# A second wait inside each pair's eight gathers, in the first layer of a graph network

## The reference

```
h   = relu(layernorm(x))
ef  = (relu(edge_attr @ We1 + be1) @ We2 + be2) * sigmoid(edge_weight @ Wt + bt)
msg = relu(concat([h[src], ef]) @ Wn1 + bn1) @ Wn2 + bn2
x   = x + (segment_sum(msg, dst) + h)                      # first layer
h   = relu(layernorm(x))
agg = segment_sum(h[src], dst)
x   = x + relu(relu((h + agg) @ W1 + b1) @ W2 + b2)        # second layer
```

## Time and profile before

| | us |
|---|---|
| median of 3 runs | 3862.44 (3859.89 to 3878.18) |
| the profiled execution: device time | 3848.36 |
| its span on the core | 3846.6 |
| mean granted TensorE clock | 0.797 |
| first gather of the program, last one | 47.7, 3797.0 |

### The profile page before, as it was taken

One profiled execution on the slowest core, in us unless ns is written; L12 is line 12 of the kernel. 1 busy time (PEld: TensorE's weight loads), 2 busy tenths in 40 slices (PEclk: granted clock), 3 DMA queues, 4 the chain that ended last, 5 costly groups with the idle time before them and its releaser, 6 DMA issues.

```text
span 3846.6 us, 58359 instructions
## 1 busy us (share of the span) xinstructions
PE 2746.8 (71%) x14587; PEld 1705.2 (44%) x14588; DVE 1970.9 (51%) x4080; ACT 1013.4 (26%) x1000; POOL 2069.2 (54%) x2109
## 2 busy tenths in 40 slices
PE   4877677767677777778777877776663766667667
PEld 3444444444344444435444444443342544455445
DVE  8654555555555555555555555564674333333333
ACT  3332333323233333323233332322231101111112
POOL 7655555555455555555555554545336455555553
PEclk8788888887888788878887887877886767777778
DMA  5433333333333333333334343333213333333331
GB/s 169 123 119 111 113 120 110 111 120 105 117 101 120 110 109 116 120 107 115 112 114 116 104 124 109 114 109 104 79 51 128 99 96 122 123 120 98 111 121 63
DMA packets 234934, 426.49 MB, mean 111 GB/s; under 512 B 86462, under 2 KB 147470, under 8 KB 234542
## 3 DMA queue, kind: packets, MB, share of 16 engines
q0 software_dynamic: 74160, 151.46, 15.3%
q1 hardware_dynamic: 109552, 178.49, 14.1%
q10 hardware_dynamic: 50928, 93.34, 6.8%
HBM read 363.64 MB, written 59.42 MB: 110 GB/s over the span
## 4 chain that ended last, share of the span: by engine, by line
issue 27%; PE 21%; SPq 20%; DVE 13%; another core or an unknown queue 10%; DVEq 7%; DMA 1%; ACT 0%; POOL 0%; ACTq 0%
SPq L486 14%; PE ps L1000 9%; PE ps L900 4%; SPq L482 3%; DVE nodes L1270 3%; PE ps L858 3%; DVEq L1194 2%; PE ps L868 2%; DVEq L1250 1%; DVE arena L1270 1%; DVEq L1267 1%; PE ps L990 1%; DVE big L1220 1%; DVE hot L1225 1%
## 5 line engine op out<-in xcount | busy, mean ns | idle before, releaser
L592 POOL DMA_INDIRECT big<-table,idx x2064 | 2001.8, 970 | 1670.8 <-issue 593.7
L900 PE MATMUL ps<-nodes 128*128 128x500 bf16 x1280 | 433.6, 460 | 324.5 <-DVE nodes L1270 191.4
L858 PE MATMUL ps<-arena,we 128*128 128x512 f32 x784 | 496.0, 762 | 28.5 <-issue 16.2
L713 ACT ACTIVATE big<-big 128x1024 f32<-128x1024 f32 x196 | 207.1, 1057 | 1151.1 <-DVE big L1220 828.3
L1270 DVE TENSOR_SCALAR nodes<-iota_k,win_off,nodes 128x500 bf16<-128x500 f16 x1280 | 461.6, 413 | 0.5 <-issue 0.5
L879 PE MATMUL ps<-hot,big 128*128 128x64 f32 x3136 | 414.2, 288 | 52.8 <-issue 28.2
L879 PEld LDWEIGHTS ps<-hot,big 128*128 128x128 f32 x3136 | 406.0, 208 | 57.6 <-issue 55.7
L1220 DVE TENSOR_TENSOR big<-ps,big 128x1024 f32<-128x1024 f32 x180 | 219.5, 1219 | 354.0 <-issue 287.4
L849 PE MATMUL ps<-arena,we 64*128 64x512 f32 x784 | 258.0, 727 | 199.9 <-DMA arena<-in_ea 187.0
L1267 DVE TENSOR_TENSOR nodes<-iota_b,nodes 128x384 bf16<-128x384 f16 (+1 forms) x492 | 245.5, 499 | 223.0 <-remote 182.6
L1202 DVE TENSOR_TENSOR acc<-ps,acc 128x128 f32 x392 | 114.1, 291 | 458.4 <-remote 398.6
(11 more groups left out here) (152 smaller groups left out, 2604.4 us busy)
## 6 DMA issues: line engine op xcount, KB each, us to landing
arena<-in_ew SPq DMA_DIRECT2D x196, 512.0 KB
arena<-in_ea SPq DMA_DIRECT2D x196, 256.0 KB
counts_d<-arena ACTq DMA_DIRECT2D x192, 245.0 KB
acc<-counts_d ACTq DMA_DIRECT2D x15, 2940.0 KB
big<-table,idx POOLq DMA_INDIRECT x2064
nodes<-table SPq DMA_DIRECT2D x2048, 0.5 KB
table<-big SPq DMA_DIRECT2D x7, 672.0 KB, 3.0
idx<-in_src SPq DMA_DIRECT2D x260, 4.0 KB
```

What stands on the lines that cost most here:

```text
L592: pool.indirect_dma_start(to(u, q, t)[0:n], None, table, bass.IndirectOffsetOnAxis(ap=idx[0:n, u, at:at + 1], axis=0))\
L858: i = pe.matmul(p_ef[q], we2[:, :], hid[:, q, :], start=True, stop=True)
L900: m = pe.matmul(to, hots[:, t, :], keys[:, t, :], start=False, stop=True, skip_group_check=True)
```

## The change

GpSimd's eight gathers of a pair are split by block. The first four are issued after the three waits of before. Ahead of the second four there is now a wait for `agg_mm >= 4 b + u - 2` and one more raising of `pairs_begun`, on which no one waits. The count P-2 is reached when TensorE has done the sums of pair P-3, in its step P. The last two bodies get no new wait; pair 195's short tile and the tile left out of the 16 special pairs are as before. The helper `gather_rest` gives way to `gather_half`. The second layer isn't touched.

```diff
+            def gather_half(b, u, q, last):
+                if last and u == RING - 1:
+                    gather_block(table0, to_rows, u, q, gathered, EDGE_TILES - (NTILE - (2 - q) * TB))
+                elif isinstance(b, int) and (b * RING + u, q) in FETCHED:
+                    gather_block(table0, to_rows, u, q, gathered, TB, (TB - 1) * q)
+                else:
+                    gather_block(table0, to_rows, u, q, gathered)
...
                     if not free:
                         pool.wait_ge(ef_mm, b * (2 * RING) + 2 * u)
                     pool.sem_inc(pairs_begun, 1)
-                    if last and u == RING - 1:
-                        gather_last(table0, to_rows, gathered)
-                    elif isinstance(b, int) and b * RING + u in dict(FETCHED):
-                        gather_rest(table0, to_rows, u, dict(FETCHED)[b * RING + u], gathered)
-                    else:
-                        gather_pair(table0, to_rows, u, gathered)
+                    gather_half(b, u, 0, last)
+                    if not free:
+                        pool.wait_ge(agg_mm, b * RING + (u - 2))
+                    pool.sem_inc(pairs_begun, 1)
+                    gather_half(b, u, 1, last)
```

More of the change, by code:

```diff
@@ L599, in gather_pair @@
                     gather_block(table, to, u, q, landed)
-            def gather_rest(table, to, u, half, landed):
-                for q in (0, 1):
-                    gather_block(table, to, u, q, landed, TB, (TB - 1) * q if q == half else None)
             def gather_last(table, to, landed):
```

## The result

The changed kernel took **3701.7 us** (median of 6 runs, 3693.1 to 3717.9), the kernel before 3861.2 us (6 runs, 3849.4 to 3878.2): a ratio of **0.959**, 95% interval 0.956 to 0.962. The forecast was 3798 with a range of 3690 to 3950. The sign is right and the time lies in the range, but the gain is 160 us where 64 were forecast.

The account below looks back on a forecast made before the run. GpSimd's gather batches were taken to hold up news between engines. 46 bodies x (2.3 us gained - 0.9 us second pauses) = 64 us, from 3848.4 to 3784, plus 14 for the median: 3798 us, range 3690 to 3950.

Parts of the forecast that it names:

- The hold: First layer: during gather batches and 1.6 to 1.9 us after, little news passes between engines; 8.2 of a light pair's 12.6 us.
- The rule of the Trainium skill: A DMA never contends with a compute engine, so gathers wouldn't make the 2.9 us gaps and a split would give nothing.
- The new wait is found unmet: Ahead of the fifth gather: news of the sums comes only once gathers stop, so GpSimd pauses 2.9 us there.
- the extra instructions are hidden: GpSimd's added wait and increment per pair hide in the 0.30 us gap between gathers; bound 110 us if not.
- The light pairs: Sums' news passes in the middle of a pair, so TensorE starts the heavy pair 4.9 us sooner.
- Second pauses: GpSimd pauses 2.9 us again at the border in one light pair of ten: 0.9 us per body, between 0 and 8.7.
- The heavy pair: Needs about 9.8 us outside holds, before and after; ends at 53.9 us after the change, 56.2 before.
- The last eight pairs: The last two bodies have no new wait and were left out of the sum: change of 0.
- Both pauses: Rival: edge products regularly unknown after the second four, light pair 15.2 us instead of 12.6; 3996 or 4115 us; chance 0.30.
- Short batches not held: Rival: half of the lone batches of four pass without a hold; about 5 us per body, 3632 us; chance 0.10.
- Nothing: Rival: sums known in time, or the pause merely moves into the pair with batches of eight; 3862 us; chance 0.17.
- the tail: Time a hold lasts after a gather batch's end: 1.6 to 1.9 us, taken as 1.7.

Follow-up runs that it names:

- e13: Changed kernel with four small GpSimd instructions, which wait for nobody, in place of the second wait: ratio 0.953.
- the fifth chip: Chip of the fifth group: kernel before 2834.6 us; changed kernel with two or seven small GpSimd instructions in place of the second wait: 1.076 and 1.262.
- e1: Changed kernel with the second wait on the sums of one pair earlier, always known already: ratio 1.002.
- e8: Changed kernel with the second wait on the products of this pair's attributes instead of the sums: ratio 1.002.
- e15: The changed kernel itself once more, on the fourth group's chip: ratio 0.955.
- e11: Changed kernel with the second wait in the three light pairs of each body alone: ratio 0.989.
- e10: Changed kernel with the second wait in the heavy pair of each body alone: ratio 0.980.
- e2: Kernel before with all eight gathers of a pair behind the sums, in place of the wait for the edge products: ratio 0.966.
- e14: Changed kernel, the heavy pair's second four gathers waiting for the end of its own counting instead of the sums: ratio 0.976.
- e9: Changed kernel with both waits in the last two bodies too: ratio 0.951.
- e12: Changed kernel without SyncE's single-row transfers and with both waits in the last two bodies too: 3561.1 us, ratio 0.939.
- e7: Kernel before with first-layer gathers of 16 rows instead of 128 from pair 4 on: ratio 1.032.
- e6: SyncE's single-row transfers left out, GpSimd gathering those tiles: kernel before 0.986, changed kernel 0.947.

## Why the prediction was right or wrong

**The hold: right.** In the changed kernel too VectorE and SyncE move together just before GpSimd resumes; SyncE's twelves stay slow; e13 shows that a stop without any news of its own is enough, and the fifth chip speaks for it from the other side: without the hold the stop is a loss. The rule of the Trainium skill that was weighed ("SBUF — State Buffer", Who interferes with whom), by which the gaps would not be of the gathers' making, gave "nothing": it doesn't cover this.

**The new wait is found unmet, and the extra instructions are hidden: right.** Gaps stand in the middle of light pairs and hardly at a border; e1 and e8 price the instructions at 0.2% with an interval around zero, where the bound was 110 us.

**The light pairs: near.** Forecast -4.9 us, with the second pauses +0.9, so -4.0; measured -2.7. *Second pauses* came out smaller than the term: besides the pairs behind a heavy one, which have both pauses as forecast (33 of 45), only 5 of 135 pairs have one in the middle and one at the border, 5 x 2.5 / 45 = 0.3 us per body for 0.9. The pauses in the middle last 2.3 to 2.7 us on average where 2.9 was taken. One thing wasn't in the sum at all: SyncE. Its fetches beside gathers are so slow that the attributes behind them came late for 8.3 us of a body, 4.0 before. The prediction had read SyncE as slow in each hold and didn't follow its queue to the attributes. In the two kernels without fetches the light pairs fell from 34.6 to 31.2 us, 3.4 less (on two chips whose kernels before differ by 0.4%). But leaving the fetches out is worth no more to the changed kernel (0.947 for 0.959) than to the one before (0.986), so it isn't shown that the later attributes cost the change much.

**The heavy pair: the step that failed.** By the prediction "it needed about 9.8 us outside holds" before, and it gave the pair the same 9.8 us outside holds after the change. Work done in a hold thus counted as nothing, and the pair grew from 18.4 to 21.0: +2.6. Measured: 19.2 to 18.0, -1.2 (18.3 in e15, on a chip where the kernel before has no profile). This term alone is 3.8 us x 46 = 175 us off; the light pairs (1.3 x 46 = 60) and the last eight pairs (27) were off to the other side, which leaves 88 of the whole error of 96.

The prediction's own rows could have told. It let the heavy pair begin at 1486.4, with the news. TensorE's rows of that pair begin earlier, inside the hold, and the counting that follows meets the next one:

```profile
1483.88 1.13 PE L849 MATMUL ps<-arena,we 64*128 64x512 f32 x4 [0.20 <-issue]
1484.94 2.06 PE L868 MATMUL ps<-wn1b,ef 128*128 128x128 f32 x16
...
1491.58 2.86 PE L900 MATMUL ps<-nodes 128*128 128x500 bf16 x6 [1.62 <-issue]
```

With the prediction's bounds of a hold (from 3.3 us after a batch's start to 1.7 us after its end) TensorE is busy for 72% of the time in holds and 79% outside them before, and for 81% and 67% after (pairs 8 to 187). Windows of a heavy pair after (us, then busy us and number of instructions for PE, PEld, DVE, ACT, POOL; clock, DMA share, GB/s), the first in a hold and the second behind it, against the earlier trace rows:

```profile
1454.60:1462.90 8.30, 7.69 (x44) 5.60 (x42) 3.77 (x9) 2.24 (x2) 4.92 (x6) 0.79 0.39 114
1462.90:1467.80 4.90, 2.55 (x7) 0.55 (x7) 4.28 (x10) 0.25 (x1) 3.05 (x4) 0.74 0.34 96
```

In this hold TensorE works for 7.69 of 8.30 us, where before it had 2.86 of 8.60. A hold stops news, not work. TensorE's timeline of that stretch, and VectorE's first row behind it:

```profile
1454.31 1.39 PE L852 MATMUL ps<-arena,we 64*128 64x512 f32 x4 [3.78 <-DMA arena<-in_ea]
1455.63 3.39 PE L871 MATMUL ps<-wn1b,ef 128*128 128x128 f32 x16
1458.86 1.90 PE L882 MATMUL ps<-hot,big 128*128 128x64 f32 x16
1460.56 0.25 PE L885 MATMUL ps<-hot_sum,ones 128*1 128x128 f32 x1
...
1460.85 1.44 PE L903 MATMUL ps<-nodes 128*128 128x500 bf16 x6
1464.96 1.14 PE L903 MATMUL ps<-nodes 128*128 128x500 bf16 x3 [2.67 <-DVE nodes L1273]
```

```profile
1463.38 0.56 DVE L1270 TENSOR_TENSOR nodes<-iota_b,nodes 128x384 bf16<-128x384 f16 x1 [5.02 <-PE ps L903]
```

From the attributes to the sums TensorE runs straight through the hold, without one wait, since what it needs was known ahead. The counting needs many exchanges between VectorE and TensorE. In the body of the earlier trace rows the batch began at the edge products, so that the counting ran into the hold and stood there. The pause now comes at the end of the sums, and the counting's remaining steps (VectorE builds matrices from 1463.38 on, and TensorE counts with them from 1464.96 on) fall into the end of the pause of 2.8 us and the head of the next batch. The stage from sums to edge products shows it: 9.1 us before, 6.6 after; 9.9 in e11, whose heavy pair has no stop, 6.2 in e10, whose heavy pair has one. e2 fits: it moves all batches behind the sums, has 84% of the gain with no split, and its stage takes 6.5 us. And e11, with no stop in the heavy pair, has just the 21.0 us that the prediction gave it: what it mis-sized is what a stop inside the heavy pair is worth. So far the failed step is shown. Why the stop is worth so much, that it takes the counting out of the hold, is argued and not shown. Two couples speak against it as the whole reason: without fetches the change leaves the heavy pair as it is (19.7 and 19.6) and the stage gets longer (8.5 to 10.5 us), with the same ratio of 0.960; and e14 keeps the second four off the counting and wins nothing by it. The higher clock is a rival that no run excludes. Where in the body the gain lands differs from kernel to kernel; that the gathers stop is what they have in common.

**The last eight pairs: not in the sum.** The free last bodies took 27 us longer. With waits there as well they take 139 to 140 us (e9, e12). The prediction had given them no change, and since kernels with the old order there vary between 140 and 168 us, the 27 us can't be put down to the change with certainty.

**The sum again.** Forecast -4.9 + 2.6 + 0.9 = -1.4 us per body, -64 us. Measured -2.7 - 1.2 = -3.9 (-4.0 unrounded), x 46 = -184, + 27 = -157 us. The time lies 12 us above the lower end of the range, which was set by the rival of the short batches; that it still fell inside, with the heavy pair's sign wrong, is luck.

**The rivals.** *Both pauses* fell: 5 pairs of 135, where it begins to decide at one light pair per body (45). *Short batches not held*: the short batches exist (76), but only around heavy pairs and fetches; its time (3632) wasn't reached. *Nothing* fell with e2 and e13. Its variant, that the pause only moves and batches stay at eight, describes what happened to the batches, and was wrong on the heavy pair.

**What stays open.** What the hold is. It goes with gather instructions of GpSimd, whatever they move (e7) and without SyncE's transfers (e6), and there was none on one chip of five. Whether a pause shorter than the tail would help where there is a hold wasn't measured.

## What to carry over

A stretch in which no engine is full and several engines with different releasers start at the same instant is worth a test with a blind pause: if the kernel gets faster by issuing less densely, the issuing holds up the news. When a stage is placed against such a hold, don't count its work as nothing: look in the trace how much of it is done there. And follow what is queued behind a slowed instruction: here the time that TensorE waited for attributes doubled, and dropping the transfers ahead of them with the waits kept to the end made the best kernel (0.939). Before such a pause is kept, time it on more than one chip: where there was no hold, it cost nearly its whole length.

## What was unexpected of the hardware

- The same program took 2834.6 us on one chip and 3785.7 to 3861.2 on the others, each time with runs within about 1% of each other. On the slow ones a register move of SyncE takes up to 1406 ns beside gathers, on the fast one 29 ns throughout.
- An indirect gather of 16 rows keeps GpSimd for 0.83 us, one of 128 rows for 0.94 us; the next follows after 0.30 us in both.
- A small wait more in each pair on GpSimd costs nothing that can be measured (1.002, 0.999 to 1.005).
